# A residual shared out to ScalarE and GpSimd, expert results stored from ScalarE's queue, gathers that wait for tile 4, and a reordered tail, in a four-stage network kernel on one Trainium2 core

## The reference

```python
x = L0_attn_x                                        # (8, 512, 128) float32
x = x + _layernorm(_L0_attn_ref(_layernorm(x), ...)) # selective state space layer
x = x + _layernorm(_L0_ffn_ref(_layernorm(x), ...))  # mixture of 8 experts, 2 per token
x = x + _layernorm(_L1_attn_ref(_layernorm(x), ...)) # gated attention in groups of 32 tokens
x = x + _layernorm(_L1_ffn_ref(_layernorm(x), ...))  # 128 -> 384 -> 128, int8 weights
```

## Time and profile before

| | us |
|---|---|
| median of 3 runs (lowest, highest) | 582.27 (581.85, 584.56) |
| the profiled execution | 578.57 |
| its span, first to last instruction | 576.8 |
| around the span | 1.77 |
| mean granted TensorE clock | 0.969 |
| TensorE busy | 484.9 (84%) |
| VectorE busy | 455.9 (79%) |
| ScalarE busy | 306.6 (53%) |
| GpSimd busy | 310.9 (54%) |

### The profile page before, as it was taken

How to read it: one execution, slowest core, us unless ns; L and a number is a source line. 1 busy time by engine, 2 the same in 40 slices (tenths; PEclk the granted TensorE clock), 3 DMA queues, 4 the chain that set the end, 5 groups by cost and what they waited for, 6 DMA issues and landing times.

```text
span 576.8 us, 11015 instructions
## 1 busy us (share of the span) xinstructions
PE 484.9 (84%) x3102; PEld 396.1 (69%) x3102; DVE 455.9 (79%) x1742; ACT 306.6 (53%) x655; POOL 310.9 (54%) x349
## 2 busy tenths in 40 slices
PE   7998998899898987678678687888888998889990
PEld 3555787697786866456555465777888897778890
DVE  3885678999898899967574467888888988799974
ACT  3767775667657562244243344565555566445531
POOL 5852553726677667657432657377787232224342
PEclk9999998999999999999798798999999999999996
DMA  7704999900000001335356764321212000000111
GB/s 192 233 2 119 286 285 285 276 6 9 20 25 15 27 11 36 91 105 173 123 166 183 218 197 147 118 56 56 73 50 63 1 2 0 2 1 20 37 38 55
DMA packets 74213, 54.87 MB, mean 95 GB/s; under 512 B 5665, under 2 KB 69665, under 8 KB 74154
## 3 DMA queue, kind: packets, MB, share of 16 engines
q1 hardware_dynamic: 69034, 41.58, 24.6%
q0 software_dynamic: 5120, 12.59, 7.5%
HBM read 19.70 MB, written 34.45 MB: 94 GB/s over the span
## 4 chain that ended last, share of the span: by engine, by line
PE 39%; issue 21%; DVE 18%; POOL 12%; ACT 5%; DMA 1%; SPq 1%; another core or an unknown queue 1%; POOLq 0%; DVEq 0%; ACTq 0%
PE ps L1907 5%; POOL z_rows L557 5%; PE ps L1909 4%; PE ps L1908 4%; POOL tails L705 2%; PE ps L2303 2%; PE ps L2369 2%; POOL work L680 2%; DVE rstats_t L1248 2%; PE ps L2228 2%; PE ps L2371 2%; DVE X L1210 1%; PE ps L2128 1%; PE ps L2394 1%; PE ps L1924 1%
## 5 line engine op out<-in xcount | busy, mean ns | idle before, releaser
L570 POOL DMA_INDIRECT shared_buf<-g_rows,back x64 | 64.1, 1001 | 37.5 <-DVE slot_g L1693 21.4
L557 POOL DMA_INDIRECT z_rows<-Z,dest x64 | 64.3, 1004 | 24.5 <-issue 16.6
L1907 PE MATMUL ps<-w_hi,ZT_hi 128*128 (+1 forms) x110 | 47.8, 435 | 18.3 <-issue 11.9
L823 ACT ACTIVATE Z<-X,shift,rstds 128x128 f32<-128x128 f32 x128 | 53.3, 484 | 11.8 <-DVE shift L1174 8.6
L1009 ACT ACTIVATE half_tanh<-ps 128x256 f32<-128x256 f32 x78 | 29.2, 384 | 53.7 <-PE ps L1909 40.7
L542 POOL TENSOR_TENSOR rstds<-vars_t,mhalf 128x4 f32<-128x4 f32 (+1 forms) x24 | 31.4, 1308 | 47.5 <-DVE vars_t L1197 24.8
L1693 DVE SCALAR_TENSOR_TENSOR slot_g<-half_tanh,ps 128x256 f32<-128x256 f32 x78 | 31.5, 416 | 29.8 <-ACT half_tanh L1009 17.5
L547 POOL TENSOR_TENSOR res_rstd<-rvar,mhalf 128x4 f32<-128x4 f32 x24 | 25.2, 1051 | 38.8 <-DVE rvar L1265 38.8
L1908 PE MATMUL ps<-w_lo,ZT_hi 128*128 (+1 forms) x110 | 41.7, 379 | 0.0
L1909 PE MATMUL ps<-w_hi,ZT_lo 128*128 (+1 forms) x110 | 41.4, 377 | 0.0
L1907 PEld LDWEIGHTS ps<-w_hi,ZT_hi 128*128 128x128 f32 x110 | 21.9, 199 | 27.5 <-issue 26.4
(11 more groups left out here) (359 smaller groups left out, 1568.3 us busy)
## 6 DMA issues: line engine op xcount, KB each, us to landing
z_rows<-zero SPq DMA_DIRECT2D x34, 512.0 KB, 6.6
g_rows<-slot_g SPq DMA_DIRECT2D x38, 256.0 KB
slot_zs<-z_rows SPq DMA_DIRECT2D x78, 64.0 KB
X<-in_x SPq DMA_DIRECT2D x4, 512.0 KB, 6.5
RES<-in_W1T SPq DMA_DIRECT2D x4, 512.0 KB, 5.6
out<-X SPq DMA_DIRECT2D x7, 256.0 KB, 2.3
z_rows<-Z,dest POOLq DMA_INDIRECT x64
shared_buf<-g_rows,back POOLq DMA_INDIRECT x64
```

Source lines behind the costliest of these rows:

```text
L557: pool.indirect_dma_start(z_rows[group(i)], bass.IndirectOffsetOnAxis(ap=dest[:, i, k, c:c + 1], axis=0), Zr[i % 4][:, c], None).then_inc( ...
L570: pool.indirect_dma_start(got[:, c, k], None, g_rows[group(i)], bass.IndirectOffsetOnAxis(ap=back[:, i, k, c:c + 1], axis=0))\
L823: act.activation(dst[:, c], X[:, i, c], ACT.Identity, bias=bias[:, c:c + 1], scale=rstd[:, c:c + 1]).then_inc(z_made, 1)
L1907: pe.matmul(dst, lh, rh, start=start, stop=False)
```

## The change

The change has six parts.

1. For the residual of stage 1 of sequences 0 to 6, VectorE no longer adds; it keeps only `constant`. ScalarE multiplies the four RES tiles by res_rstd at the end of step 4(i+1) + 2 (it waits for GpSimd's power, then increments the new semaphore `scaled`). GpSimd adds the four tiles in one instruction at the start of the next step, ahead of its other work there, and increments `x_new`. Sequence 7 stays as it was.
2. The 40 stores of slot tiles leave SyncE's queue for ScalarE's: after the tanh of each even tile j > 0 ScalarE waits for g of tile j - 1 and stores j - 2 and j - 1; at a group's last tile it also waits for that tile's own g. SyncE only loads, in plain order; `LATE_LOADS` goes.
3. The last 11 scatters start one or two tiles of stage B later. GpSimd's power of sequence 7's statistics comes one scatter earlier.
4. Gather t waits for tile 2t + 5 of group 1 counting from one, where it waited for 2t + 2. `power(2, 0)` comes ahead of gather 12's wait. All of `MOE_AT`, and the statistics and residual steps at fixed tiles of group 1, move by two tiles.
5. TensorE leaves out the five identity products from step 32 on (three gates), and the rank products come after the expert product of their tile, not before.
6. In the tail `lastD(6)` comes after the statistics of sequence 7's second half.

```diff
-        SCATTER_TILE = (..., (5, 1, 7), (5, 2, 9), (5, 3, 11), (6, 0, 13), (6, 1, 15),
-                        (6, 2, 17), (6, 3, 19), (7, 0, 21), (7, 1, 23), (7, 2, 25), (7, 3, 27))
-        LATE_LOADS = {33: 0, 35: 1, 37: 2, 38: 3}
+        SCATTER_TILE = (..., (5, 1, 9), (5, 2, 11), (5, 3, 13), (6, 0, 15), (6, 1, 17),
+                        (6, 2, 19), (6, 3, 20), (7, 0, 22), (7, 1, 24), (7, 2, 26), (7, 3, 28))
-        MOE_AT = (8, 10, 12, 14, 16, 18, 20, 22, 24, 26, 28, 30)
+        MOE_AT = (10, 12, 14, 16, 18, 20, 22, 24, 26, 28, 30, 32)
 # SyncE
-            for n, (g, q) in enumerate(QUADS):
-                for j in quad_tiles(g, q):
-                    if j % 2 == 1 or j == GTILES[g] - 1:
-                        store_pair(g, j - j % 2, 1 + j % 2)
-                    if g == 0 and j in LATE_LOADS:
-                        load_quad(QUADS.index((1, LATE_LOADS[j])))
-                    if j == min(4 * q + 2, GTILES[g] - 1) and n + AHEAD < len(QUADS) and QUADS[n + AHEAD][0] == g:
-                        load_quad(n + AHEAD)
+            for n in range(AHEAD, len(QUADS)):
+                load_quad(n)
 # GpSimd, gate
+                    if place == 0 and at == 3 and i < SEQS - 1:
+                        pool.wait_ge(scaled, (i + 1) * CH)
+                        pool.tensor_tensor(X[:, i], X[:, i], RES[:, i], ALU.add).then_inc(x_new, 1)
 # GpSimd, stage B
-                pool.wait_ge(g_made, GTILES[0] + 2 * t + 2)
+                pool.wait_ge(g_made, GTILES[0] + 2 * t + 5)
 # ScalarE, gate
+                    if place == 1 and at == 2 and i < SEQS - 1:
+                        act.wait_ge(rpow_made, i + 1)
+                        for c in range(CH):
+                            act.activation(RES[:, i, c], RES[:, i, c], ACT.Identity, scale=res_rstd[:, i, c:c + 1])\
+                               .then_inc(scaled, 1)
 # ScalarE, stage B
+            def store_pair(g, j, many):
+                r = ring(g, j)
+                act.wait_ge(g_made, GFIRST[g] + j + many)
+                act.dma_start(g_rows[g][j * P:(j + many) * P, :].rearrange("(k p) d -> p k d", p=P),
+                              slot_g[:, r % 8:r % 8 + many]).then_inc(slot_stored[r // 2 % 4], 16)
...
                     slot_tanh(GFIRST[g] + j)
+                    if j % 2 == 0 and j > 0:
+                        store_pair(g, j - 2, 2)
+                    if j == GTILES[g] - 1:
+                        store_pair(g, j - j % 2, 1 + j % 2)
-                    if g == 1 and j == 30:
+                    if g == 1 and j == 32:
                         z(2, 0)
 # VectorE, x_add
+                if stage == 1 and i < SEQS - 1:
+                    constant(stage, i)
+                    return
 # VectorE, tail
-                if half == 0:
-                    lastD(SEQS - 2)
             rbn_aggr(4, i)
+            lastD(SEQS - 2)
 # TensorE, gate
-                        for k in range(5):
-                            pe.matmul(bank(2)[:, 3 * P:4 * P], ident[:], ident[:], start=True, stop=True)
+                        if step < NT:
+                            for k in range(5):
+                                pe.matmul(bank(2)[:, 3 * P:4 * P], ident[:], ident[:], start=True, stop=True)
```

More of the change, by code:

```diff
@@ L733, in _ @@
                     res_power(1, SEQS - 1)
-                if (i, c) == (5, 1):
+                if (i, c) == (5, 0):
                     power(1, SEQS - 1)
             for t in range(4 * CH):
-                pool.wait_ge(g_made, GTILES[0] + 2 * t + 2)
+                if t == 12:
+                    power(2, 0)
+                pool.wait_ge(g_made, GTILES[0] + 2 * t + 5)
                 gather(t)
@@ L740, in _ @@
                     res_power(2, 0)
-                if t == 12:
-                    power(2, 0)
                 if t == 13:
@@ L967, in stepA @@
                         set_of(ACT.Exp)
+                gate(i * CH + c, 1)
                 if i == 1 and c == 2:
@@ L2242, in _ @@
                             gate(NT + j // 2 - 1, 1)
-                        elif j > 2:
-                            gate(NT + j // 2 - 1, 2)
                     slot_h(GFIRST[g] + j, n, j, experts[j - 4 * q])
+                    if g == 0 and 2 < j and j % 2 == 1 and NT + j // 2 - 1 < GATE_END:
+                        gate(NT + j // 2 - 1, 2)
                     if g == 0 and j == 0:
```

27 lines of the change are left out of this document (11 added, 16 removed).

## The result

The changed kernel takes 583.63 us, median of 20 runs (581.53 to 589.04); the kernel before took 581.43 in the 20 runs beside it. The ratio is 1.0049, with a 95% interval of 1.0026 to 1.0071: slower by some 2.9 us, where 0.2 us faster had been forecast. The two medians differ by 2.2 us, because some executions of most kernels take over 1.5% longer than the fastest and the ratios leave them out; five of the profiles are of such executions (before_again, residual_dve_again, residual_dve_gathers_old, residual_dve_hi_first, z_before_tail). The time lies inside the forecast's range, but the change moved the other way. The loss is small against the noise: further down the unchanged kernel came out 0.4% faster than itself. What carries the argument are the traces. The profiled execution has a span of 579.8 us, 3.0 longer than before.

What follows compares the result with a forecast made beforehand. No single engine was taken as the bound; each part was priced in its stage. 3.3 - 1.0 - 2.5 + 0.5 + 0.7 + 0 - 1.2 = -0.2 gave 582.1 us from 582.27, range for 8 in 10 575.0 to 588.5.

Steps and rivals of the forecast that it cites:

- earlier loads: Between the expert groups: with stores off SyncE's queue, loads wait only for scatters; TensorE's first transpose at 303.8, not 304.8: -1.0.
- The credit of 1.5: Early stage A: VectorE's freed additions shorten sequences 0, 1 and 2 by 0.5 us each, -1.5 (0 to -3.6).
- The addition at sequence 2: Stage A: GpSimd is idle there (4.04 us before 122.42), so its addition for sequences 0 to 2 is free.
- The wait at steps 19 and 23: Stage A, sequences 3 and 4: VectorE stands 2.3 us for GpSimd's late addition, 1.6 us each reach TensorE.
- Sequences 5 and 6: Late stage A: order of work is looser, so half of GpSimd's addition counts, 0.65 and 0.5 us.
- The gathers, -2.5: Group 1 of stage B: spreading the gathers removes nearly half of 5.55 us TensorE idle time, -2.5 (-6 to +1).
- The stores, +0.5: Stage B: ScalarE's 40 stores and waits for g are mostly covered, costing +0.5 us (0 to +4).
- The seam, +0.7: End of group 1 to stage C: ScalarE's last stores and wait for g precede its stage C work, +0.7 (+0.3 to +1.4).
- The tail, -1.2: Kernel's end: sequence 7's second-half statistics start at once, with lastD(6) under the power, -1.2 us (0 to -2.3).
- GpSimd becomes the bound of stage A: Rival, stage A: GpSimd's delay carries between sequences through scatters and power, +8.8 instead of +3.3, 587.6 us; chance 0.24.
- VectorE was the bound of early stage A: Rival, stage A: 1.2 us gained in each of three sequences, -1.7 instead of +3.3, 577.1 us; chance 0.08.
- The stalls were queues and bursts: Rival, stage B: spreading the gathers removes the joint stalls, -7.7 instead of -2.5, 576.9 us; chance 0.27.

Runs made afterwards that it cites:

- before_again: The kernel before, unchanged, run and profiled a second time: ratio 0.996 (0.9923 to 0.9998).
- residual_dve_again: The changed kernel with part 1 undone (VectorE adds the residual), run again on the first sort of chip: ratio to the kernel before 0.9943.
- residual_dve_gathers_old: The changed kernel with the residual on VectorE and part 4 undone (gathers wait for tile 2t+2, old MOE_AT): ratio to the kernel before 1.0089.
- residual_dve_hi_first: The changed kernel with the residual on VectorE and ScalarE's first stage C work ahead of group 1's last two stores: ratio to the kernel before 1.0015.
- z_before_tail: The kernel before with part 6 alone, the tail: ratio 0.9982 (0.9951 to 1.0013).
- after_add_before_scatters: The changed kernel with GpSimd's addition moved to the end of the step before, ahead of the scatters: ratio to the kernel before 1.0158.
- before_plus_residual: The kernel before with part 1 alone (ScalarE scales, GpSimd adds): ratio 1.0076 (1.0033 to 1.0119).
- x_residual_first_two: The changed kernel with part 1 for sequences 0 and 1 only, the others on VectorE: ratio to the kernel before 1.0108.
- after_add_in_four: The changed kernel with GpSimd's addition cut into four 128x128 instructions: ratio to the kernel before 1.0025 (0.9989 to 1.0061).
- x_idle_add: The kernel before plus a GpSimd addition whose result nobody reads, at the new addition's place; VectorE's addition kept: ratio 1.0139.
- x_idle_memset: The kernel before plus a GpSimd memset of a dead RES tile at the new addition's place; VectorE's addition kept: ratio 1.0026.
- x_hi_first_again: The changed kernel with the residual on VectorE and ScalarE's first stage C work ahead of the last two stores, run again: ratio to the kernel before 1.0112.
- before_plus_gathers: The kernel before with part 4 alone (gathers wait for tile 2t+5, combination and statistics two tiles later): ratio 0.9994.
- before_plus_stores: The kernel before with part 2 alone (stores by ScalarE, SyncE only loads), old scatter times: ratio 0.9968 (0.9935 to 1.0002).

## Why the prediction was wrong, and where it was right

Two steps failed. In stage A the prediction priced GpSimd's addition by VectorE's wait for X, as free for sequence 2, and against a credit for VectorE's freed time; the runs show GpSimd's queue up to its power as the path, a held VectorE instruction at sequence 2, and no credit. In stage B it counted on 3.5 us from earlier loads and spread gathers, less 0.5 for the stores; 0.9 came in the profiles, and by the experiments neither term brought it. The seam and the tail came out nearly as forecast.

**Stage A, +3.3 forecast, about +5.8 measured.** Four kernels with GpSimd's addition in all sequences have stage A at 192.5 to 194.1 (one of them, after_add_before_scatters, on the second sort of chip), seven with VectorE's alone on the first sort of chip at 186.2 to 188.7; the means, 193.4 and 187.6, are 5.8 apart. In the steps of the sum:

- The credit of 1.5 for VectorE's freed time early: 0.0 in before_plus_residual (89.20 against 89.19) and in x_residual_first_two (sequences 0 and 1). A busy share of 23.02 of 24.40 was no bound there; the step is refuted.
- The addition at sequence 2, priced as free because GpSimd is idle there: +1.43. GpSimd had the time, but its reading holds VectorE (2.04 us for 0.43). The rule stood in the prediction as a sentence and had no term in the sum. after_add_in_four and the pair x_idle_add and x_idle_memset show it. With the credit before it that is 2.9 us, somewhat more than the stage's whole error of 2.5.
- The wait at steps 19 and 23, forecast 2.3 us, measured 2.30 and 2.29; forecast cost 1.6 a sequence, measured 1.25 and 1.40. Size nearly right, mechanism wrong, so the size was luck. I let the wait for X carry the cost and put GpSimd's power "beside, not on top". after_add_before_scatters took the wait away and the cost stayed, and x_idle_add made the cost without the wait: it is GpSimd's queue up to its power that late stage A waits for, and each microsecond put in front of it counts nearly in full. The row of 198.44 was in hand; what it needed was the row behind it, VectorE waiting for it.
- Sequences 5 and 6, 1.15 forecast, 1.1 to 2.4 measured (28.26 against 25.85 to 27.16 in the seven on the first sort). The granted clock of this stretch is 0.76 in the changed kernel, in before_plus_residual and in x_idle_add, and 0.87 to 1.00 in those seven. But after_add_before_scatters took 28.34 at 0.94; how much of the loss is the clock stays open.
- ScalarE's scaling, 1.65 estimated, took 1.26 us; its 0.45 at step 10 did not show (exp 11 to 12, where step 10 ends, took 9.94 against 9.93).

**Stage B, -1.0 - 2.5 + 0.5 = -3.0 forecast.** Measured 0.9 between the two first profiles; by the means of first sort chips, 122.0 in four kernels with the new stage B against 124.2 in four with the old, 2.1. The direction was right, the terms were not. TensorE's first transpose of group 1 did not come 1.0 earlier against the first tanh: 63.55 us behind it, against 61.64 in the first profile of the kernel before and 64.16 and 63.16 in the others. The sum itself was short: it gave "checks and loads" 3.7 us, but the kernel before has 5.3 from the end of the store, 299.56, to 304.82, and x_hi_first_again has 4.1 between the scatter's landing and the transpose. I had the last scatters follow back to back to 298.0, but the one before last waited for its tile until 303.07, after a stall in which ScalarE stood for 4.53 us, VectorE for 3.48 and TensorE for 2.15 (GpSimd, changed kernel):

```profile
299.14 0.96 POOL L543 DMA_INDIRECT z_rows<-Z,dest  x1 [0.30 <-issue]
303.07 0.96 POOL L543 DMA_INDIRECT z_rows<-Z,dest  x1 [2.97 <-DVE slot_g L1702]
304.34 0.96 POOL L543 DMA_INDIRECT z_rows<-Z,dest  x1 [0.30 <-issue]
```

The gathers, -2.5: tanh 39 to 54 got 2.2 us shorter (20.45 against 22.67), and before_plus_gathers alone shows nothing in the sum; with ScalarE's stores in place its worth stays open (residual_dve_gathers_old). The stores, +0.5, were more likely the gain instead (before_plus_stores, some 3.5 us in stage B, one profile), on one sort of chip. Part 5, forecast at 0, and part 3 were not run alone, so their shares aren't known.

**The seam, +0.7**: 10.06 against 9.31, +0.75; TensorE's wait grew from 1.41 to 2.00 us. The cause, ScalarE's last stores, is shown by residual_dve_hi_first (9.34). With the residual on VectorE it cost 1.5; why more than with part 1 isn't shown.

**The tail, -1.2**: 13.14 to 11.88, -1.26. As forecast the power starts earlier and an instruction beside GpSimd's addition is stretched; only it is now the next one, L1897 (VectorE and GpSimd, changed kernel; the first is the one that was 1.22 us long in the earlier trace rows):

```profile
570.90 0.15 DVE L1895 SCALAR_TENSOR_TENSOR rtemp<-means,res_rstd 128x4 f32<-128x4 f32 x1
571.06 1.26 POOL L765 TENSOR_TENSOR X<-X,slot_g 128x512 f32<-128x512 f32 x1 [0.30 <-DVE slot_g L1862]
571.09 1.25 DVE L1897 TENSOR_TENSOR res_shift<-offset,rtemp 128x4 f32<-128x4 f32 x1
```

**The rivals.** "GpSimd becomes the bound of stage A" came nearest: +8.8 there against 6.2 measured without the episode's luck, and with the right mechanism, GpSimd's delay carried through scatters and power. Its sizes were too large: 2.3 for each of sequences 3 and 4 (1.25 and 1.40), and 1.8 for ScalarE's scaling (nothing). It had a chance of 0.24. "VectorE was the bound of early stage A" has fallen. "The stalls were queues and bursts" has no support from part 4 alone and is open for part 2 and for the two together.

**Left open.** What the stalls of all engines in stage B are. They are there on one sort of chip (stage B 121 to 125 us) and nearly gone on the other (104 to 111) for kernels with the same order of work, so that order can't be the whole of it. Nor is it shown why ScalarE's stores seem to help stage B on the first sort and not on the second.

## What to carry to other kernels

Before work is moved to an engine "with room", look in the trace whether its queue runs without idle time up to something that another engine waits for, even by 0.24 us: there it can be the bound, whatever its busy share is (17.69 of 24.90 us here). An instruction that reads on GpSimd can have a second price, a held two-input VectorE instruction. An extra instruction that nobody needs, once one that reads and once one that only writes, measures both prices before anything is moved. And cut traces at instructions that all kernels share, since the luck of one execution (1.7 us in a clock episode, up to 7 in stage 0) is larger than most parts of a change.

## What the runs showed of the hardware

Two sorts of chips ran the same kernel in 581 to 582 and in 557 to 558 us. Parts 2 to 6 together were 0.6% faster than the kernel before on a chip of the first sort, and, with ScalarE's last stores moved, 0.15% (no more than noise) and 1.1% slower on two of the second. A two-input VectorE instruction was held from 0.43 to 2.18 us by a 1.27 us GpSimd addition whose record starts 0.62 us after its own, and not by a 0.54 us memset at the same place. A VectorE tensor_scalar of 0.17 us, with one tile as its input, took 1.17 us beside such an addition and 0.42 beside such a memset; two VectorE instructions with one input in SBUF and one in PSUM kept their 0.42 us beside an addition. Cutting a 128x512 addition on GpSimd into four 128x128 ones took it from 1.27 to 1.69 us, and the VectorE instruction beside it from 2.04 to 0.57.
